# Graph layer in fp32 by split matmuls: early pieces loaded in halves, residual loads moved, and second-half pieces loaded two by two

## The chip, the cores and the metric

The kernel runs on one core of one Trainium2 chip. The metric is the device time of one execution in microseconds; less is better. The kernel before takes 717.71 us (median of 3 runs, 717.27 to 717.86).

## The reference

```python
h = jnp.maximum(_layernorm(x, axis=-1), 0.0)          # x: 8192 x 128, eps 1e-5
x = x + (0.9 * (adj @ h) + 0.1 * L0_gnn_h)            # adj: 8192 x 8192, all float32
```

The work is one product of an 8192 x 8192 matrix with an 8192 x 128 matrix in float32. `adj` alone is 268 MB and is read once.

## The kernel before

The output is computed transposed: 16 chunks of 512 output rows, each chunk one PSUM bank of 128 x 512. `adj` arrives in 256 **pieces** of 128 x 2048 floats (1 MB), numbered q. Pieces 0 to 127 are **wide**: a piece is one block of 128 nodes for four of the first eight chunks, so that block k needs only h of block k, and two pieces use one block. Pieces 128 to 255 are **tall**: a piece is four blocks for one chunk, 16 pieces to a chunk. All of h is made during the wide half.

A float32 product is made from three faster ones. For every piece from 2 on, ScalarE writes `a_hi`, the piece rounded to fp32r (L270), and VectorE writes `a_lo = raw - a_hi` (L316, `low_a`). h is split in the same way into `h_hi` and `h_lo`. TensorE then does 12 matmuls of 512 columns for a piece: four of `h_hi` with `a_hi`, four of `h_lo` with `a_hi`, four of `h_hi` with `a_lo` (L406, L412, L417 in the wide half; L428, L429, L433 in the tall one). Pieces 0 and 1 are multiplied in float32 straight from `raw` (L395).

Everything is written out by hand, with one queue of instructions for each engine and semaphores between them:

- SyncE (SP) issues every transfer, in one queue. `raw` has 6 slots. The load of piece q waits until `a_lo` of piece q - 6 is written (L183, `lo_ready`), since both splits read `raw`. Between the pieces SP issues the loads of x (one for a unit of four blocks, 256 KB, at the pieces in `LOAD_X_AT`), the loads of the residual inputs x and L0_gnn_h for chunk n (512 KB, `load_residual`), and the stores.
- `a_hi` and `a_lo` have 3 slots. ScalarE starts on piece q once TensorE is done with piece q - 3 (`piece_used`).
- The residual load n goes to the one buffer `res_sb`; its issue waits until the sum of load n - 1 is made on VectorE (`add_residual`). `RES_LOAD_AT` and `RES_SUM_AT` give the piece at which SP issues the load and the piece after which VectorE makes the sum. SP stands about 6 pieces ahead of VectorE.
- VectorE makes the layernorm statistics after the pieces in `STATS_AT`, in groups of blocks (`GROUPS`: 1, 3, 4, 4, 4, then 8 blocks); GpSimd makes `rstd`; ScalarE scales and clips h (`scale_unit`) and copies it to `h_hi` (`high_h`), VectorE makes `h_lo` (`low_h`).
- `PARTS` says which pieces are loaded and split in parts: 0 and 1 in four, 2 to 9 in two. A part has a semaphore of its own, so that work starts when a part has landed.
- A finished chunk is scaled, added to its residual (`finish`) and stored; `FINISH` lists chunk and piece.

Of the kernel before, what the change touches and what calls it, by code (L numbers as in the profile page):

```python
# [27 lines left out]
PARTS = {0: 4, 1: 4}  # L28
PARTS.update({_q: 2 for _q in range(2, 10)})
PART_SEMS = sum(PARTS.values())  # L30

# [4 lines left out]
GROUPS = [(0, 1), (1, 4), (4, 8), (8, 12), (12, 16)] + [(_b, _b + 8) for _b in range(16, BLOCKS, 8)]  # L36
# [3 lines left out]
STATS_AT, AGGREGATE_AT, SHIFT_AT, SCALE_AT, LOW_H_AT, LOAD_X_AT = {}, {}, {}, {}, {}, {}  # L40
for _g, (_a, _b) in enumerate(GROUPS):
    if _g < 3:
        continue
    _single = _b - _a == UNIT
    _d = 5 if _g == 3 else 2 * _a - 12 if _single else 2 * _a - 19
    for _k in range(_a, _b):
        STATS_AT.setdefault(_d + _k - _a, []).append(_k)
    _end = _d + _b - _a
    AGGREGATE_AT[_end] = _g
    SHIFT_AT[_end + 1] = _g  # L50
    for _u in range(_a // UNIT, _b // UNIT):
        _s = _end + 3 + 2 * (_u - _a // UNIT)
        SCALE_AT[_s], SCALE_AT[_s + 1] = (_u, 0), (_u, 1)
        LOW_H_AT[_s + 2] = _u
        LOAD_X_AT[_d - 1 + 4 * (_u - _a // UNIT)] = _u
# [46 lines left out]
def build(nc, x, adj_wide, adj_tall, res, out):  # L102
# [4 lines left out]
    with ctx:  # L107
# [19 lines left out]
        exponent = sb("exponent", [P, 2 * UNIT])  # L127
        rstd = sb("rstd", [P, BLOCKS])
        shift = sb("shift", [P, BLOCKS])
        warm = sb("warm", [P, SEG], bf16)  # L130
# [3 lines left out]
        part_landed = [sem(f"part_landed{i}") for i in range(PART_SEMS)]  # L134
# [40 lines left out]
        def _(sp):  # L175
# [28 lines left out]
            load_piece(1)  # L204
            load_x(2, UNIT, 2 * UNIT)
            for q in range(NATIVE, PIECES):
# [3 lines left out]
                load_piece(q)  # L210
# [25 lines left out]
        def _(act):  # L236
# [12 lines left out]
            def scale_unit(u, half):  # L249
# [15 lines left out]
            for q in range(NATIVE, PIECES):  # L265
# [6 lines left out]
                if q == 4:  # L272
                    scale_unit(1, 0)
                if q == 5:
                    scale_unit(1, 1)
                if q in SCALE_AT:
                    scale_unit(*SCALE_AT[q])

        @block.vector
        def _(dve):  # L280
# [74 lines left out]
            dve.wait_ge(x_landed[2], 16)  # L355
# [111 lines left out]
```

## Time and profile before

| | before |
|---|---|
| median of 3 runs | 717.71 us |
| the profiled execution | 718.35 us |
| its span (first to last instruction) | 716.6 us |
| TensorE busy | 707.0 us (99%) |
| VectorE busy | 625.0 us (87%) |
| ScalarE busy | 521.3 us (73%) |
| moved by DMA | 285.73 MB, mean 399 GB/s |
| granted TensorE clock, mean | 1.000 |

The profiled execution took 718.35 us, of which 716.6 us are its span and 1.75 us lie around it; it is 0.64 us above the median. TensorE's busy time is modelled from pipelined matmuls: a matmul row says 0.39 us, but they follow each other every 0.227 us. So its gaps are better read from the start times of pieces than from the busy time.

### The profile page before, as it was taken

How to read it: one execution, taken by the hardware profiler on the slowest of the kernel's cores; microseconds unless marked ns; L12 is line 12 of the kernel's file. 1: busy time of each engine (PE TensorE's matmuls, PEld its weight loads, DVE VectorE, ACT ScalarE, POOL GpSimd, SP SyncE). 2: the span in 40 equal slices, each digit the busy share in tenths (PEclk: the TensorE clock that was granted, in tenths of full speed). 3: DMA queues.
4: the chain of work that ended last, by engine and by line, in shares of the span. 5: the costliest groups of instructions: out<-in, count | busy, mean ns of one | idle time of the engine just before them, and what ended most of it. 6: DMA issues, size and time to landing. Idle time of an engine off the chain costs nothing.

```text
span 716.6 us, 7886 instructions
## 1 busy us (share of the span) xinstructions
PE 707.0 (99%) x3076; PEld 575.3 (80%) x3076; DVE 625.0 (87%) x462; ACT 521.3 (73%) x342; POOL 27.6 (4%) x17
## 2 busy tenths in 40 slices
PE   7999999999999999999999999999999999999998
PEld 2777888888888888888888888888888888888886
DVE  3879998998999989998888888888888889888985
ACT  3878877869688796877767676676767767676773
POOL 1001102001020100200000000000000000000000
DMA  8999999999999999999999999999999999999991
GB/s 291 411 418 420 403 419 419 415 422 414 421 411 422 416 415 402 420 421 412 383 398 409 387 395 378 403 397 388 413 387 406 423 418 413 420 415 425 420 422 75
DMA packets 46117, 285.73 MB, mean 399 GB/s; under 512 B 5120, under 2 KB 5632, under 8 KB 14592
## 3 DMA queue, kind: packets, MB, share of 16 engines
q1 hardware_dynamic: 46080, 285.23, 98.2%
q8 instruction: 24, 0.39, 0.2%
q14 instruction: 13, 0.11, 0.0%
HBM read 281.02 MB, written 4.19 MB: 398 GB/s over the span
## 4 chain that ended last, share of the span: by engine, by line
PE 88%; DMA 4%; DVE 3%; issue 2%; ACT 1%; SPq 1%; POOL 0%; DVEq 0%; ACTq 0%
PE acc L428 16%; PE acc L429 16%; PE acc L433 16%; PE acc L417 13%; PE acc L412 13%; PE acc L406 13%; DMA raw<-wide_dram 4%; DVE a_lo L316 2%; SPq L190 1%; ACT a_hi L270 1%; POOL rstd L232 0%; ACT h_full L239 0%; DVE stats L282 0%; SPq L179 0%; DVE h_lo L308 0%
## 5 line engine op out<-in xcount | busy, mean ns | idle before, releaser
L316 DVE TENSOR_TENSOR a_lo<-raw,a_hi 128x2048 fp32r<-128x2048 f32 (+1 forms) x262 | 581.3, 2224 | 65.3 <-ACT a_hi L270 64.8
L270 ACT ACTIVATE a_hi<-raw 128x2048 fp32r<-128x2048 f32 (+1 forms) x262 | 487.7, 1865 | 175.3 <-PE acc L433 90.4
L428 PE MATMUL acc<-a_hi,h_hi 128*128 128x512 f32 x512 | 199.2, 389 | 0.0
L429 PE MATMUL acc<-a_hi,h_lo 128*128 128x512 f32 x512 | 199.2, 389 | 0.0
L406 PE MATMUL acc<-a_hi,h_hi 128*128 128x512 f32 x504 | 135.9, 390 | 3.0 <-ACT a_hi L270 3.0
L417 PE MATMUL acc<-a_lo,h_hi 128*128 128x512 f32 x504 | 135.8, 391 | 1.2 <-DVE a_lo L316 0.8
L433 PE MATMUL acc<-a_lo,h_hi 128*128 128x512 f32 x512 | 136.8, 389 | 0.0
L412 PE MATMUL acc<-a_hi,h_lo 128*128 128x512 f32 x504 | 134.8, 389 | 0.0
L406 PEld LDWEIGHTS acc<-a_hi,h_hi 128*128 128x128 f32 x504 | 94.1, 188 | 25.2 <-issue 2.9
L417 PEld LDWEIGHTS acc<-a_lo,h_hi 128*128 128x128 f32 x504 | 93.9, 188 | 23.8 <-DVE a_lo L316 4.6
L429 PEld LDWEIGHTS acc<-a_hi,h_lo 128*128 128x128 f32 x512 | 96.1, 188 | 20.0
L433 PEld LDWEIGHTS acc<-a_lo,h_hi 128*128 128x128 f32 x512 | 96.1, 188 | 20.0
L428 PEld LDWEIGHTS acc<-a_hi,h_hi 128*128 128x128 f32 x512 | 96.1, 188 | 19.9
L412 PEld LDWEIGHTS acc<-a_hi,h_lo 128*128 128x128 f32 x504 | 94.6, 188 | 19.8
L232 POOL TENSOR_TENSOR rstd<-var_eps,exponent 128x8 f32<-128x8 f32 (+3 forms) x11 | 26.9, 2443 | 267.0 <-DVE var_eps L295 267.0
L239 ACT ACTIVATE h_full<-x_sb,shift,rstd 128x128 f32<-128x128 f32 x63 | 27.2, 480 | 9.4 <-DVE shift L301 9.4
L282 DVE BATCH_NORM_STATS2 stats<-x_sb 128x6 f32<-128x128 f32 x64 | 17.6, 286 | 9.7 <-DMA x_sb<-x_dram 9.7
L335 DVE SCALAR_TENSOR_TENSOR finished<-acc,residual 128x512 f32<-128x512 f32 (+1 forms) x17 | 11.0, 653 | 3.8 <-issue 3.8
L308 DVE TENSOR_TENSOR h_lo<-h_full,h_hi 128x512 fp32r<-128x512 f32 x16 | 10.9, 683 | 0.0
L324 DVE SCALAR_TENSOR_TENSOR residual<-res_sb 128x512 f32<-128x512 f32 x16 | 10.9, 682 | 0.0
L246 ACT ACTIVATE h_hi<-h_full 128x512 fp32r<-128x512 f32 x16 | 10.1, 633 | 0.6
L301 DVE SCALAR_TENSOR_TENSOR shift<-mean_var,rstd 128x8 f32<-128x8 f32 (+2 forms) x10 | 1.6, 164 | 9.3 <-POOL rstd L232 9.3
(15 smaller groups left out, 26.9 us busy)
## 6 DMA issues: line engine op xcount, KB each, us to landing
raw<-tall_dram SPq DMA_DIRECT2D x128, 1024.0 KB, 8.7
raw<-wide_dram SPq DMA_DIRECT2D x118, 1024.0 KB, 9.8
raw<-wide_dram SPq DMA_DIRECT2D x16, 512.0 KB, 12.6
res_sb<-res_dram SPq DMA_DIRECT2D x16, 512.0 KB, 5.6
x_sb<-x_dram SPq DMA_DIRECT2D x15, 256.0 KB, 10.2
out_dram<-finished SPq DMA_DIRECT2D x15, 256.0 KB, 9.1
raw<-wide_dram SPq DMA_DIRECT2D x8, 256.0 KB, 6.4
out_dram<-finished SPq DMA_DIRECT2D x2, 128.0 KB, 1.8
```

The costliest lines, as they stand in the source:

```text
L232: nc.gpsimd.tensor_tensor(rstd[:, a:b], var_eps[:, a:b], exponent[:, 0:b - a], ALU.pow).then_inc(rstd_ready, 1)
L239: last = nc.scalar.activation(h_full[:, in_h(k), :], x_sb[:, in_x(k), :], ACT.Relu, bias=shift[:, k:k + 1], scale=rstd[:, k:k + 1])
L270: nc.scalar.activation(a_hi[:, q % SPLIT_SLOTS, cols], raw[:, q % RAW_SLOTS, cols], ACT.Copy).then_inc(hi_ready, 1)
L282: return nc.vector.bn_stats(stats[:, k, :], x_sb[:, in_x(k), :])
L316: nc.vector.tensor_tensor(a_lo[:, q % SPLIT_SLOTS, cols], raw[:, q % RAW_SLOTS, cols], a_hi[:, q % SPLIT_SLOTS, cols].bitcast(fp32), ALU.s ...
L335: nc.vector.scalar_tensor_tensor(out=finished[:, n % 2, cols], in0=acc[:, c % WIDE, cols], scalar=1.0 - ALPHA, in1=residual[:, n % RES_RIN ...
L406: nc.tensor.matmul(acc[:, quad * QUAD + j, :], h_hi[:, k, :], a_hi[:, slot, cols], start=False, stop=False)
L412: nc.tensor.matmul(acc[:, quad * QUAD + j, :], h_lo[:, k, :], a_hi[:, slot, cols], start=False, stop=False)
L417: last = nc.tensor.matmul(acc[:, quad * QUAD + j, :], h_hi[:, k, :], a_lo[:, slot, cols], start=False, stop=(k == BLOCKS - 1))
L428: nc.tensor.matmul(bank, h_hi[:, k, :], a_hi[:, slot, cols], start=(k == 0), stop=False)
L429: nc.tensor.matmul(bank, h_lo[:, k, :], a_hi[:, slot, cols], start=False, stop=False)
L433: last = nc.tensor.matmul(bank, h_hi[:, k, :], a_lo[:, slot, cols], start=False, stop=(k == BLOCKS - 1))
```

## The change

1. **Parts.** Pieces 0 to 23 are loaded in halves and split into `a_hi` in halves; the quarters of pieces 0 and 1 are gone. The halves lie in an array of their own, in which each is one stretch of memory. VectorE makes `a_lo` in halves only up to piece 5 (`LOW_PARTS`), and in one pass from piece 6 on.
2. **x and h.** All groups have four blocks. The first load of x behind block 3 moves from ahead of piece 2 to ahead of piece 4, the next ones come at pieces 5, 13, 21 and so on, every eight pieces. `high_h` moves one piece behind the scaling, `h_hi` and `h_lo` included for unit 1.
3. **Residuals.** The first eight loads move from pieces 12, 24, ..., 96 to 44, 54, ..., 114, with the sum at the next piece number on VectorE; the later ones come four pieces earlier, their sums six.
4. **Pairs.** In the tall half one transfer of 2 MB brings pieces q and q + 1 (q even) into two neighbouring slots, with one semaphore. It waits for `a_lo` of piece q - 5.
5. **Warm-up.** TensorE's 12 warm-up matmuls of 512 columns become 15 of 256.

```diff
-PARTS = {0: 4, 1: 4}
-PARTS.update({_q: 2 for _q in range(2, 10)})
+EARLY, EARLY_LOW = 24, 6
+PARTS = {_q: 2 for _q in range(EARLY)}
+LOW_PARTS = {_q: 2 for _q in range(EARLY_LOW)}
...
-    RES_LOAD_AT[12 + 12 * _n if _n < RES_RING else _at - 5] = _n
-    RES_SUM_AT[20 + 12 * _n if _n < RES_RING else _at - 2] = _n
-WARM_UP = 12
+    RES_LOAD_AT[44 + 10 * _n if _n < RES_RING else _at - 9] = _n
+    RES_SUM_AT[45 + 10 * _n if _n < RES_RING else _at - 8] = _n
+WARM_UP = 15
...
+        def load_of(q):
+
+            return q if q < WIDE_PIECES else q - q % 2
+
         def wait_landed(engine, q, i):
             if q in PARTS:
-                engine.wait_ge(part_landed[part_number(q, i)], 16)
+                engine.wait_ge(part_landed[q % RAW_SLOTS][i], 16 * landed_turn(q))
             else:
-                engine.wait_ge(raw_landed[q % RAW_SLOTS], 16 * landed_turn(q))
+                engine.wait_ge(raw_landed[load_of(q) % RAW_SLOTS], 16 * landed_turn(load_of(q)))
...
+            def load_two(q):
+                slot = q % RAW_SLOTS
+                sp.wait_ge(lo_ready, low_through(q + 1 - RAW_SLOTS))
+                sp.dma_start(raw[:, slot:slot + 2, :], adj_tall[(q - WIDE_PIECES) // 2, :, :, :]
+                             ).then_inc(raw_landed[slot], 16)
...
-                load_piece(q)
+                if q < WIDE_PIECES:
+                    load_piece(q)
+                elif q % 2 == 0:
+                    load_two(q)
...
             def low_a(q):
-                for i, cols in parts(q):
-                    dve.wait_ge(hi_ready, split_through(q, i))
+                for i, cols in low_parts(q):
+                    dve.wait_ge(hi_ready, split_through(q, i if q in LOW_PARTS else None))
```

**SP's queue at the start.** These are SP's transfers before, from the first one to the second residual load; `128x512`, `128x1024` and `128x2048` on `raw` are a quarter, a half and a whole piece.

```order
L190 DMA raw<-wide_dram 128x512 x4
L179 DMA x_sb<-x_dram 128x512
L190 DMA raw<-wide_dram 128x1024 x4
L179 DMA x_sb<-x_dram 128x512
L190 DMA raw<-wide_dram 128x1024 x12
L190 DMA raw<-wide_dram 128x2048
L179 DMA x_sb<-x_dram 128x512
L190 DMA raw<-wide_dram 128x2048
L179 DMA x_sb<-x_dram 128x512
L190 DMA raw<-wide_dram 128x2048
L195 DMA res_sb<-res_dram 128x1024
L190 DMA raw<-wide_dram 128x2048 x3
```

The first row above is piece 1, the third pieces 2 and 3. This is the same place in the changed queue, from the load of x blocks 1 to 3 to the last half.

```order
L194 DMA x_sb<-x_dram 128x384
L213 DMA raw<-early_dram 128x1024 x6
L194 DMA x_sb<-x_dram 128x512
L213 DMA raw<-early_dram 128x1024 x2
L194 DMA x_sb<-x_dram 128x512
L213 DMA raw<-early_dram 128x1024 x16
L194 DMA x_sb<-x_dram 128x512
L213 DMA raw<-early_dram 128x1024 x16
L194 DMA x_sb<-x_dram 128x512
L213 DMA raw<-early_dram 128x1024 x6
```

Ahead of piece 2 there is one load of x fewer, ahead of piece 13 still one fewer, and no residual load stands among the first 44 pieces.

**VectorE, pieces 3 to 6.** Before, each `a_lo` is written in two halves (`128x1024`), pieces 3, 4 and 5 in the first row and piece 6 in the third:

```order
L316 TENSOR_TENSOR a_lo<-raw,a_hi 128x1024 x6
L282 BN_STATS stats<-x_sb 128x6
L316 TENSOR_TENSOR a_lo<-raw,a_hi 128x1024 x2
L308 TENSOR_TENSOR h_lo<-h_full,h_hi 128x512
L282 BN_STATS stats<-x_sb 128x6
```

Now, from piece 4 on:

```order
L337 TENSOR_TENSOR a_lo<-raw,a_hi 128x1024 x2
L322 SCALAR_TENSOR_TENSOR shift<-mean_var,rstd 128x4
L337 TENSOR_TENSOR a_lo<-raw,a_hi 128x1024 x2
L303 BN_STATS stats<-x_sb 128x6
L337 TENSOR_TENSOR a_lo<-raw,a_hi 128x2048
```

Piece 6, the last row, is now one pass that needs both halves of `a_hi`.

**SP's queue in the tall half.** Before, around the residual load for finish 8 (issued behind piece 188):

```order
L190 DMA raw<-tall_dram 128x2048 [waits lo_ready] x4
L195 DMA res_sb<-res_dram 128x1024 [waits residual_ready]
L190 DMA raw<-tall_dram 128x2048 [waits lo_ready] x3
L199 DMA out_dram<-finished 128x512 [waits finished_ready]
L190 DMA raw<-tall_dram 128x2048 [waits lo_ready] x4
```

Now, around the same load (issued behind the pair 184, 185):

```order
L199 DMA raw<-tall_dram 128x4096 [waits lo_ready] x5
L218 DMA res_sb<-res_dram 128x1024 [waits residual_ready]
L222 DMA out_dram<-finished 128x512 [waits finished_ready]
L199 DMA raw<-tall_dram 128x4096 [waits lo_ready] x3
L218 DMA res_sb<-res_dram 128x1024 [waits residual_ready]
```

A load is now two pieces (`128x4096`), and the residual load and a store stand side by side, where three single pieces stood between them.

## Rows read from the trace of the kernel before

**Rows 1.** Page, part 1: TensorE's busy time, share of the span, instructions.

```profile
PE 707.0 (99%) x3076; PEld 575.3 (80%) x3076; DVE 625.0 (87%) x462; ACT 521.3 (73%) x342; POOL 27.6 (4%) x17
```

**Rows 2.** Five stretches: busy us (x instructions) by engine, clock, DMA share, GB/s.

```profile
0.00:10.00 10.00, 8.41 (x20) 3.02 (x20) 2.11 (x11) 1.28 (x1) 1.33 (x7) 1.00 0.71 207
10.00:20.00 10.00, 6.92 (x21) 3.82 (x22) 6.09 (x16) 6.13 (x8) 2.24 (x2) 1.00 1.03 399
100.00:150.00 50.00, 50.00 (x223) 41.39 (x222) 46.49 (x45) 39.13 (x29) 3.62 (x1) 1.00 1.01 417
400.00:450.00 50.00, 50.00 (x222) 41.42 (x221) 43.33 (x21) 34.91 (x19) 0.00 (x0) 1.00 1.01 387
650.00:700.00 50.00, 50.00 (x222) 41.42 (x221) 43.20 (x21) 34.80 (x20) 0.00 (x0) 1.00 1.02 422
```

**Rows 3.** TensorE in order of time: start us, us, line, shape, count.

```profile
16.31 0.70 PE L406 MATMUL acc<-a_hi,h_hi 128*128 128x512 f32 x2 [2.09 <-ACT a_hi L270]
...
39.87 1.07 PE L406 MATMUL acc<-a_hi,h_hi 128*128 128x512 f32 x4
...
82.17 1.07 PE L406 MATMUL acc<-a_hi,h_hi 128*128 128x512 f32 x4
...
710.49 0.39 PE L428 MATMUL acc<-a_hi,h_hi 128*128 128x512 f32 x1
```

**Rows 4.** ScalarE's splits that waited for a landing; idle before, releaser in brackets.

```profile
15.11 1.06 ACT L270 ACTIVATE a_hi<-raw 128x1024 fp32r<-128x1024 f32 x1 [1.75 <-DMA raw<-wide_dram]
...
16.37 1.06 ACT L270 ACTIVATE a_hi<-raw 128x1024 fp32r<-128x1024 f32 x1 [0.21 <-DMA raw<-wide_dram]
...
18.93 1.06 ACT L270 ACTIVATE a_hi<-raw 128x1024 fp32r<-128x1024 f32 x1 [0.21 <-DMA raw<-wide_dram]
...
20.89 1.06 ACT L270 ACTIVATE a_hi<-raw 128x1024 fp32r<-128x1024 f32 x1 [0.90 <-DMA raw<-wide_dram]
...
43.86 1.92 ACT L270 ACTIVATE a_hi<-raw 128x2048 fp32r<-128x2048 f32 x1 [1.24 <-DMA raw<-wide_dram]
...
47.59 1.91 ACT L270 ACTIVATE a_hi<-raw 128x2048 fp32r<-128x2048 f32 x1 [1.04 <-DMA raw<-wide_dram]
...
60.69 1.92 ACT L270 ACTIVATE a_hi<-raw 128x2048 fp32r<-128x2048 f32 x1 [0.56 <-DMA raw<-wide_dram]
...
63.18 1.92 ACT L270 ACTIVATE a_hi<-raw 128x2048 fp32r<-128x2048 f32 x1 [0.57 <-DMA raw<-wide_dram]
```

**Rows 5.** Waits, whole run: us in total, times, longest; SPq is SyncE's queue.

```profile
ACT a_hi L270 <- DMA raw<-tall_dram: 9.7, 12, 1.2
...
SPq L190 <- DVE a_lo L316: 509.8, 228, 3.6
SPq L195 <- DVE residual L324: 59.0, 13, 6.7
```

**Rows 6.** Single loads issued at 346, 365, 644 us: last number is us to landing.

```profile
raw<-tall_dram SPq DMA_DIRECT2D x1, 1024.0 KB, 6.3
...
raw<-tall_dram SPq DMA_DIRECT2D x1, 1024.0 KB, 5.6
...
raw<-tall_dram SPq DMA_DIRECT2D x1, 1024.0 KB, 12.4
```

**Rows 7.** Piece 253 from split to matmul.

```profile
699.87 1.92 ACT L270 ACTIVATE a_hi<-raw 128x2048 fp32r<-128x2048 f32 x1 [0.80 <-PE acc L433]
...
701.82 2.29 DVE L316 TENSOR_TENSOR a_lo<-raw,a_hi 128x2048 fp32r<-128x2048 f32 x1 [0.43 <-ACT a_hi L270]
...
705.05 0.39 PE L428 MATMUL acc<-a_hi,h_hi 128*128 128x512 f32 x1
```

**Rows 8.** Head: work of VectorE and ScalarE between the pieces.

```profile
16.20 2.49 DVE L316 TENSOR_TENSOR a_lo<-raw,a_hi 128x1024 fp32r<-128x1024 f32 x2 [0.28 <-ACT a_hi L270]
...
23.14 0.86 ACT L239 ACTIVATE h_full<-x_sb,shift,rstd 128x128 f32<-128x128 f32 x2
...
26.70 0.63 ACT L246 ACTIVATE h_hi<-h_full 128x512 fp32r<-128x512 f32 x1
```

More of the change, by code:

```diff
@@ L25 @@
 RAW_SLOTS, SPLIT_SLOTS = 6, 3
[L28 to L30 removed]
+EARLY, EARLY_LOW = 24, 6
+PARTS = {_q: 2 for _q in range(EARLY)}
+LOW_PARTS = {_q: 2 for _q in range(EARLY_LOW)}
+PART = PIECE // 2
 UNIT = 4
@@ L35 @@
 X_RING, H_RING = 6, 4
[L36 to L55, printed above, removed]
+GROUPS = [(0, 1), (1, UNIT)] + [(_b, _b + UNIT) for _b in range(UNIT, BLOCKS, UNIT)]
+LOAD_X_AT = {4: 1}
+STATS_AT, AGGREGATE_AT, SHIFT_AT = {3: list(range(UNIT, 2 * UNIT))}, {3: 2}, {4: 2}
+SCALE_AT, HIGH_H_AT, LOW_H_AT = {5: (1, 0), 6: (1, 1)}, {6: 1}, {7: 1}
+for _u in range(2, UNITS):
+    _d = UNIT * QUADS * _u - 11
+    LOAD_X_AT[_d] = _u
+    for _k in range(UNIT):
+        STATS_AT[_d + _k] = [_u * UNIT + _k]
+    AGGREGATE_AT[_d + 4] = SHIFT_AT[_d + 5] = _u + 1
+    SCALE_AT[_d + 7], SCALE_AT[_d + 8] = (_u, 0), (_u, 1)
+    HIGH_H_AT[_d + 9] = LOW_H_AT[_d + 10] = _u
 FINISH = [(0, WIDE_PIECES), (1, WIDE_PIECES + 3)]
@@ L88, in split_through, with low_parts, low_through, low_part_of @@
     return sum(PARTS.get(k, 1) for k in range(NATIVE, q)) + own
+def low_parts(q):
+    n = LOW_PARTS.get(q, 1)
+    width = PIECE // n
+    return [(i, slice(i * width, (i + 1) * width)) for i in range(n)]
+def low_through(q, i=None):
+    own = LOW_PARTS.get(q, 1) if i is None else i + 1
+    return sum(LOW_PARTS.get(k, 1) for k in range(NATIVE, q)) + own
 def part_of(q, seg):
     return seg * PARTS.get(q, 1) // QUAD
+def low_part_of(q, seg):
+    return seg * LOW_PARTS.get(q, 1) // QUAD
 def pieces_of_chunk(c):
@@ L126, in build @@
         var_eps = sb("var_eps", [P, BLOCKS])
-        exponent = sb("exponent", [P, 2 * UNIT])
+        exponent = sb("exponent", [P, UNIT])
         rstd = sb("rstd", [P, BLOCKS])
         shift = sb("shift", [P, BLOCKS])
-        warm = sb("warm", [P, SEG], bf16)
+        warm = sb("warm", [P, SEG // 2], bf16)
         acc = ctx.enter_context(nc.psum_tensor("acc", [P, WIDE, SEG], fp32))
         x_landed = [sem(f"x_landed{n}") for n in range(UNITS + 1)]
-        part_landed = [sem(f"part_landed{i}") for i in range(PART_SEMS)]
+        part_landed = [[sem(f"part_landed{s}_{i}") for i in range(2)] for s in range(RAW_SLOTS)]
         raw_landed = [sem(f"raw_landed{s}") for s in range(RAW_SLOTS)]
@@ L156, in landed_turn @@
         def landed_turn(q):
-            return sum(1 for k in range(q % RAW_SLOTS, q + 1, RAW_SLOTS) if k not in PARTS)
+            return sum(1 for k in range(q % RAW_SLOTS, q + 1, RAW_SLOTS) if (k in PARTS) == (q in PARTS))
+        def load_of(q):
+            return q if q < WIDE_PIECES else q - q % 2
         def wait_landed(engine, q, i):
             if q in PARTS:
-                engine.wait_ge(part_landed[part_number(q, i)], 16)
+                engine.wait_ge(part_landed[q % RAW_SLOTS][i], 16 * landed_turn(q))
             else:
-                engine.wait_ge(raw_landed[q % RAW_SLOTS], 16 * landed_turn(q))
+                engine.wait_ge(raw_landed[load_of(q) % RAW_SLOTS], 16 * landed_turn(load_of(q)))
         def in_x(k):
@@ L203, in _ @@
             load_x(1, 1, UNIT)
-            load_piece(1)
-            load_x(2, UNIT, 2 * UNIT)
-            for q in range(NATIVE, PIECES):
+            for q in range(1, PIECES):
                 if q in LOAD_X_AT:
@@ L354, in _ @@
             make_shift(1)
-            dve.wait_ge(x_landed[2], 16)
-            for k in range(UNIT, 2 * UNIT):
-                last = statistics(k)
-            last.then_inc(stats_ready, 1)
-            aggregate(2)
             low_h(0)
@@ L389, in _ @@
             for _ in range(WARM_UP):
-                nc.tensor.matmul(acc[:, WIDE - 1, :], warm[:, 0:P], warm[:, :], start=True, stop=True)
+                nc.tensor.matmul(acc[:, WIDE - 1, 0:SEG // 2], warm[:, 0:P], warm[:, :], start=True, stop=True)
             pe.wait_ge(first_h_ready, 1)
@@ L453 @@
         "x_dram": np.ascontiguousarray(x.reshape(BLOCKS, P, F).transpose(1, 0, 2)),
-        "wide_dram": adj_wide,
+        "early_dram": adj_early,
+        "wide_dram": np.ascontiguousarray(adj_wide[EARLY:]),
         "tall_dram": adj_tall,
```

36 lines of the change are left out of this document (15 added, 21 removed).

## The prediction, on record before the run

> **What bounds the kernel now.** I read the page first. TensorE is busy for 99% of the span [rows 1], so only two things can be won: the time before its matmuls run back to back, and the tail. The windows show where it is not full: 8.41 and 6.92 us of 10 in the first two stretches of 10 us, then 50.00 of 50 [rows 2]. The DMA tells the other half: it moves 207 GB/s in the first 10 us, 399 in the next, later up to 422, always with a busy share near 1. It is close to its own limit, so both limits must be followed.
>
> Next the start times of pieces on TensorE [rows 3]. The last piece (255) starts at 710.49, piece 24 at 82.17: 628.32 us for 231 pieces, 2.720 us each. That is 12 matmuls at 0.227 us, and nothing is lost there. Ahead of it something is. Piece 2 starts at 16.31 and piece 10 at 39.87; eight pieces need 21.76 us, so 1.80 us are lost. From piece 10 to 24 it is 42.30 against 14 x 2.72 = 38.08: 4.22 us lost. So the head costs 16.31 us to its first split matmul and 6.02 us of stalls; this is all that the change can win from. The tail behind the last piece is not touched.
>
> ScalarE says what the head waits for [rows 4]. Each of these splits starts as its data land. Landings give the price of a transfer in a full queue: a half 16.37 - 15.11 = 1.26 us, a whole piece 63.18 - 60.69 = 2.49, a piece and a residual load 47.59 - 43.86 = 3.73, so the residual 1.24; a half and a load of x 20.89 - 18.93 = 1.96, so x 0.70. A piece needs 2.49 us of DMA and 2.72 of TensorE: once the head is over, DMA gains 0.23 us per piece. The head is bound by landings.
>
> **The change, part by part.** *Start.* One load of x fewer stands ahead of piece 2: -0.70 us. The quarters of pieces 0 and 1 (2 MB) become halves. No row has the price of a quarter in a full queue; the first 10 us move half of what later ones do [rows 2], but most of that is the start itself. From below it is nothing, from above the 2 MB at 207 instead of 399 GB/s would be 5 us. I take 0.5, since the halves at 1.26 us are only 1% over a whole piece and a row of half that length should be a few per cent over. Piece 2 then starts 1.2 us earlier, at 15.1. The warm-up costs nothing: TensorE waited 2.09 us for ScalarE ahead of piece 2 [rows 3], and float32 matmuls that run slower in the head are hidden up to that.
>
> *Pieces 2 to 9.* Their landings move with the start, but the second load of x comes ahead of piece 5 and not 11, so from piece 5 to 10 only 0.5 us is left of the 1.2. And the low split is one pass from piece 6 on. A pass of a half costs 2.49 / 2 = 1.25 us [rows 8], a whole one 2.29 [rows 7], and the whole one starts only when both halves of `a_hi` are made. I follow the queues. The second half of piece 2 lands at 16.37 - 1.2 = 15.2; eight halves and two loads of x later, at 26.7, that of piece 6. ScalarE has scaled two blocks (0.86, [rows 8]) behind piece 5 and ends `a_hi` of piece 6 near 28.1; the low pass ends near 30.5. TensorE started piece 6 near 27.6 and wants `a_lo` 1.81 us later, at 29.4: 1.1 us lost. For piece 7 there are 0.86 for two blocks and a copy of four more ahead of `a_hi`: 0.8 lost. For piece 8 VectorE has the low part of h as well: 0.4. With 0.85, 0.3 and 0.5 for the landings of the halves of pieces 2, 4 and 5, the stretch loses 3.9 us where 1.80 are lost now: +2.1.
>
> *Pieces 10 to 23.* The residual load at piece 12 is gone (1.24), the one at 24 too, and one load of x by piece 13 (0.70), another by 16. Piece 13 landed at 47.59 and lands near 47.59 - 1.2 - 1.24 - 0.70 + 0.2 = 44.7 (the 0.2 for halves instead of whole pieces). It now starts 1.97 us after its landing, at 49.56. Following TensorE's own pace from piece 10 (near 40.8) piece 13 starts at 49.0, more than 4 us after its landing. The landings drop out as the bound, and the gap grows by 0.23 us a piece. Of the 4.22 us I keep 0.4 for hitches of VectorE, which has many small passes: -3.8. Groups of four blocks instead of eight add only small instructions to engines that are 73 and 87% busy [rows 1]. The sum for the head is -1.2 + 2.1 - 3.8 = -2.9 us.
>
> *Residuals later on.* SP stood still for 59.0 us, in 13 waits of up to 6.7, because a residual load waited for the sum of the one before [rows 5]. With the sum right behind, this wait is gone. TensorE lost nothing by it after piece 24, so it is worth nothing by itself, but the queue stays fuller. In the wide half eight loads, one per 10 pieces instead of 12, need 10 x 2.49 + 1.24 + 1.25 x 0.70 = 27.0 us of DMA per 27.2 of TensorE. That just fits.
>
> *Pairs.* What a load may take is read at the end [rows 7]. ScalarE starts piece 253 at 699.87, once piece 250 is done; VectorE ends its low pass at 704.11; TensorE starts it at 705.05. So a low pass ends 0.94 us ahead of its piece's start, and ScalarE wants a piece 5.18 us ahead of it. Piece q is issued when the low pass of q - 6 ends, and is wanted 6 x 2.72 + 0.94 - 5.18 = 12.1 us later. A pair is issued one piece later and its even piece is wanted at the same time: 9.4 us. Another 2.7 us may pass until TensorE stands still, since ScalarE and VectorE are ahead. Single loads took from 5.6 to 12.4 us, the long ones late in the run [rows 6]; already now ScalarE waits 12 times for tall loads, 9.7 us in all [rows 5]. A pair has 2.49 us more to move: 8.1 at best.
>
> Three pairs fill the slots. Two slots are filled again after its landing, `a_hi` (1.92), two low passes (4.58) and about 0.1; with 8.1 to land this is 14.7 us, and it must go into 6 x 2.72 = 16.32. In the stretch from piece 184 to 247, a residual load and a store (half its size, 0.62) come every eight pieces: 1.86 x 6 / 8 = 1.4 us more, 16.1 in all. It fits by 0.2 us. Before, each slot was released alone and held less. If a landing takes 6.3 for a single piece, as another row has it, the sum is 16.8, 0.5 too much, and 64 pieces are 10.7 rounds: +5.3 us. So the price lies between 0 and 5.3; the row of 5.6 is the nearest to an empty queue, but residual load and store come at once, 1.86 us in a round that has 0.2 to spare on average, so I take +1.0.
>
> The Trainium skill speaks to this in "DMA: Bandwidth & Descriptors", section "Anatomy of one DMA": a fixed cost near 2.0 us plus the bytes at 436 GB/s, so that large transfers are better used. By it a 1 MB load takes 4.4 us and a pair 6.8, as an estimate. The shortest row here is 1.2 us over that, so I do not use it; by it pairs would cost nothing and the sum would be 714.8. Against the change speaks the section on why a DMA increments its semaphore by 16: only the full count says that data are there. This is what takes the even piece's head start away, and the 9.4 us above are worked out with it.
>
> **Sum.** -2.9 + 1.0 = -1.9 us. The profiled execution took 718.35 with a span of 716.6; it would take 716.45 with a span of 714.7. The median is 0.64 lower: 717.71 - 1.9 = 715.8.
>
> **The rivals.** *Pairs cost nothing* (22%): the transfer of 2 MB lands in 8.1 us or less. For it: the row of 5.6, and that DMA kept 422 GB/s to the end [rows 2]. It gives 714.8; with a start that gains 2 us instead of 1.2, 714.0. *Pairs give all of the gain back* (17%): the rounds are 0.2 to 0.3 us too long, 2 to 3.5 us of stalls: 717 to 718.3. *Slower* (16%): pairs land in 8.8 us or more. It decides from about 8.7 us on (16.7 a round, 0.4 too much, +4.1). Place: TensorE's first matmuls of even pieces from 202 on, waiting for ScalarE, and it for the DMA. For it: single loads took 10 to 12.4 us there. Against it: these are queue, and a shallower queue is what pairs have. It gives 719.9 to 721. *The head's gain does not come* (7%): the later start of `a_lo` costs as much as the landings give, so 717.5. The forecast itself, 715.0 to 716.9, has 38%.
>
> **How the numbers follow.** The bound for faster and slower is 0.2%, 1.44 us, about what a measurement of this kernel can tell: below 716.3 and above 719.1. Faster: 22 for the first rival and 28 of the forecast's 38, 0.50. Slower: 16, and 6 of the cases between, 0.22. Same: 0.28. The range leaves out one in ten on each side: 713.9, the first rival with a better start, to 720.0 within the slower one.
>
> **What would show it.** Right: piece 24 starts near 79.3 on TensorE; stalls of about 1 us at pieces 7 and 8 from VectorE's low pass; no wait for `wide_dram` after piece 12; SP's wait for the residual sum almost zero; pair landings of 8 to 10 us, waits of ScalarE for `tall_dram` above 9.7 us in total, and TensorE's idle time behind piece 200 about 1 us. Wrong: if piece 24 starts later than 81, the head failed; if pieces 184 to 255 take more than 196.8 us (72 x 2.72 = 195.8), pairs cost more than I took.

## The result, and the profile after

The changed kernel takes 723.51 us (median of 4 runs, 721.73 to 724.97) against 717.77 (717.27 to 717.86): a ratio of 1.008, 95% interval 1.0057 to 1.0104. It is slower, where 1.9 us faster was forecast. Its runs also lie further apart: 3.2 us from the lowest to the highest, where those of before span 0.6. The profiled execution took 721.73 us, its span is 719.9; it is the fastest of the four, 1.8 us under the median.

The page of the changed kernel, where it answers to [rows 1], [rows 5] and [rows 6]: busy times; GB/s in 40 slices of 18 us; ScalarE's split, with its idle time and what ended it; the transfers, with the median from issue to landing.

```profile
PE 709.8 (99%) x3079; PEld 574.1 (80%) x3079; DVE 622.7 (86%) x470; ACT 518.3 (72%) x356; POOL 40.6 (6%) x23
...
GB/s 343 410 408 413 419 420 419 421 419 417 421 420 420 419 419 420 419 421 422 381 396 384 383 390 392 392 388 400 421 416 405 423 371 410 409 369 393 382 393 108
...
L293 ACT ACTIVATE a_hi<-raw 128x2048 fp32r<-128x2048 f32 (+1 forms) x276 | 485.3, 1778 | 185.5 <-DMA raw<-tall_dram 104.3
...
raw<-tall_dram SPq DMA_DIRECT2D x64, 2048.0 KB, 10.0
...
res_sb<-res_dram SPq DMA_DIRECT2D x16, 512.0 KB, 11.1
```

The rate holds 417 to 422 GB/s from the fifth slice to the end of the wide half. Where the tall half begins it falls to 381 to 400, and the later slices but the last lie between 369 and 423. The fall is no sign of a slow DMA: a piece of 1.049 MB every 2.720 us is 386 GB/s, and that is all that a full TensorE takes there. The kernel before moved 387 from 400 to 450 us [rows 2]. ScalarE's idle time now ends mostly with a landing of a tall pair. A pair needs 10.0 us from issue to landing.

TensorE in order of time, as in [rows 3]: piece 2, the `a_lo` matmuls of pieces 6 and 7, and the first rows of pieces 10, 24, 184 and 255.

```profile
12.49 0.70 PE L418 MATMUL acc<-a_hi,h_hi 128*128 128x512 f32 x2
...
27.27 1.19 PE L429 MATMUL acc<-a_lo,h_hi 128*128 128x512 f32 x4 [0.58 <-DVE a_lo L337]
...
30.60 1.20 PE L429 MATMUL acc<-a_lo,h_hi 128*128 128x512 f32 x4 [0.30 <-DVE a_lo L337]
...
37.36 1.07 PE L418 MATMUL acc<-a_hi,h_hi 128*128 128x512 f32 x4
...
75.68 1.07 PE L418 MATMUL acc<-a_hi,h_hi 128*128 128x512 f32 x4
...
510.88 0.39 PE L440 MATMUL acc<-a_hi,h_hi 128*128 128x512 f32 x1
...
713.80 0.39 PE L440 MATMUL acc<-a_hi,h_hi 128*128 128x512 f32 x1
```

Read against 2.720 us a piece: piece 2 starts at 12.49 instead of 16.31. From 2 to 10 TensorE takes 24.87 us, 3.11 more than 21.76. From 10 to 24 it takes 38.32, 0.24 more than 38.08. Piece 24 starts 6.49 us earlier than before. From 24 to 184 it is 435.20 us for 160 pieces, 2.720 each and no loss. From 184 to 255 it is 202.92 us for 71 pieces that need 193.12: **9.80 us lost**, all of it behind piece 184, in the stretch with the residual loads. The sum -6.49 + 9.80 = +3.31 us is the difference of the spans (719.9 - 716.6 = 3.3).

Waits of the changed kernel over the whole run (total, times, longest), against [rows 5]:

```profile
ACT a_hi L293 <- DMA raw<-tall_dram: 104.3, 57, 4.1
...
ACT a_hi L293 <- DMA raw<-early_dram: 8.0, 25, 1.0
...
SPq L218 <- DVE residual L345: 0.8, 3, 0.3
```

ScalarE waits 57 times for tall landings, 104.3 us, where it was 12 times and 9.7. SP's wait for the residual sum is gone: 0.8 us where it was 59.0.

Three stretches of the changed kernel, in the columns of [rows 2]:

```profile
0.00:10.00 10.00, 7.84 (x26) 4.28 (x27) 2.44 (x13) 1.87 (x3) 1.97 (x8) 1.00 0.81 290
...
450.00:500.00 50.00, 50.00 (x223) 41.39 (x221) 42.21 (x21) 34.06 (x19) 0.00 (x0) 1.00 1.00 393
...
600.00:650.00 50.00, 48.51 (x205) 37.24 (x203) 40.50 (x22) 32.44 (x18) 0.00 (x0) 1.00 0.99 400
```

The first 10 us now move 290 GB/s (207 before). From 450 to 500 TensorE is full at 393 GB/s; from 600 to 650 it is busy for 48.51 of 50 and does 205 matmuls where 222 fit.

### The profile page after: what moved, and what is told of

Its sections match the earlier page's. It is cut to its first block, busy times and chain, and to the rows that moved or that the text cites. A ratio compares the mean times of both kernels' runs of the same rounds, so it can differ in the third digit from the quotient of the medians.

```text
span 719.9 us, 7866 instructions
## 1 busy us (share of the span) xinstructions
PE 709.8 (99%) x3079; PEld 574.1 (80%) x3079; DVE 622.7 (86%) x470; ACT 518.3 (72%) x356; POOL 40.6 (6%) x23
## 4 chain that ended last, share of the span: by engine, by line
PE 68%; DMA 16%; DVE 8%; issue 4%; ACT 3%; SPq 1%; DVEq 0%
PE acc L429 15%; PE acc L418 15%; PE acc L424 15%; DMA raw<-tall_dram 14%; PE acc L445 8%; PE acc L440 7%; PE acc L441 7%; DVE a_lo L337 7%; ACT a_hi L293 3%; DMA raw<-early_dram 2%; SPq L213 1%; DVE finished L356 0%; DVE residual L345 0%; SPq L194 0%; ACT h_full L263 0%
## 5 line engine op out<-in xcount | busy, mean ns | idle before, releaser
L293 ACT ACTIVATE a_hi<-raw 128x2048 fp32r<-128x2048 f32 (+1 forms) x276 | 485.3, 1778 | 185.5 <-DMA raw<-tall_dram 104.3
L256 POOL TENSOR_TENSOR rstd<-var_eps,exponent 128x4 f32<-128x4 f32 (+2 forms) x17 | 40.1, 2357 | 279.3 <-DVE var_eps L316 279.3
L329 DVE TENSOR_TENSOR h_lo<-h_full,h_hi 128x512 fp32r<-128x512 f32 x16 | 10.8, 677 | 2.1 <-ACT h_hi L270 2.1
L322 DVE SCALAR_TENSOR_TENSOR shift<-mean_var,rstd 128x4 f32<-128x4 f32 (+1 forms) x16 | 2.6, 161 | 10.9 <-POOL rstd L256 10.9
## 6 DMA issues: line engine op xcount, KB each, us to landing
x_sb<-x_dram SPq DMA_DIRECT2D x15, 256.0 KB, 11.2
```

Of the source, the lines that this page charges most:

```text
L256: nc.gpsimd.tensor_tensor(rstd[:, a:b], var_eps[:, a:b], exponent[:, 0:b - a], ALU.pow).then_inc(rstd_ready, 1)
L293: nc.scalar.activation(a_hi[:, q % SPLIT_SLOTS, cols], raw[:, q % RAW_SLOTS, cols], ACT.Copy).then_inc(hi_ready, 1)
```

## The experiments

All ratios are to the kernel before, run beside it on the same chip; its median was 717.87 to 718.51 us.

**The pairs alone undone** (a_singles): each tall piece by its own transfer and into its own slot.

```diff
-                elif q % 2 == 0:
-                    load_two(q)
+                load_piece(q)          # 1 MB, waits for the low pass of q - 6
```

> The changed kernel with the pairs alone undone: in the tall half each piece comes by a transfer of 1 MB into its own slot, issued when the low pass of piece q - 6 is done. Theory (the pairs alone cost the time, about 10 us behind piece 128, and the other edits win 6.5 us in the head): 711 to 712 us, no stall of TensorE behind piece 24. Rival (the faster head and the moved residual loads have used up what DMA had to spare, and pairs are only where it shows): 715 to 718 us, with stalls behind piece 184.

712.33 us (712.32 to 712.40), ratio 0.9922 (0.9907 to 0.9937). The theory holds: the other four edits win 5.6 us (the kernel before took 717.98 beside it) and the pairs cost 11.2. The rival, that the faster head used up DMA's reserve, falls.

**What of the pair costs: the late issue, the common landing, or both.** Three kernels keep transfers of 1 MB and take on one trait of the pair, or two.

```diff
 a_late: both transfers issued when the low pass of q - 5 is done; each piece usable by itself
+                sp.wait_ge(lo_ready, low_through(q + 1 - RAW_SLOTS))
+                for k in (q, q + 1):
+                    sp.dma_start(raw[:, k % RAW_SLOTS, :], adj_tall[k - WIDE_PIECES, :, :]
+                                 ).then_inc(raw_landed[k % RAW_SLOTS], 16)
 a_lump: each issued at its own time; the even piece waits for the odd one too
+                if q >= WIDE_PIECES and q % 2 == 0:
+                    engine.wait_ge(raw_landed[(q + 1) % RAW_SLOTS], 16 * landed_turn(q + 1))
 a_latelump: both edits
```

> The changed kernel, but the two pieces of a pair come by two transfers of 1 MB, issued one behind the other at the moment of the pair (low pass of q - 5), each with its own semaphore and usable by itself. Theory that the later issue is what costs: 717 to 721 us, nearly all of the loss. Theory that the common landing costs (the even piece can't be used until the odd one is there): 711 to 713 us. Theory that the transfer of 2 MB with rows of 16 KB is itself slow: 711 to 713 us.

> The changed kernel, but each tall piece comes by its own transfer of 1 MB, issued at its own time (low pass of q - 6), while ScalarE waits for both pieces of a pair before it starts on the even one. Theory of the common landing: ScalarE starts each even piece up to 2.5 us later, two slots come free late together, 714 to 719 us. Theory of late issue, or of a slow transfer of 2 MB: 711 to 713 us, since TensorE's 2.7 us of cover hold.

> The changed kernel with everything of the pairs but the transfer: two transfers of 1 MB (rows of 8 KB) are issued one behind the other when the low pass of q - 5 is done, and ScalarE waits for both before it starts on the even piece. Each of the two waits alone cost nothing (712.3 and 712.4). Theory that together they make a round of three pairs too long (the step of the prediction: 14.7 us and more in 16.3): 717 to 723 us, ScalarE waiting for tall loads about 100 us in all. Rival, the form of the transfer costs: 712 to 714 us.

The late issue alone takes 712.32 us (0.9921, 0.9906 to 0.9936). The common landing alone takes 712.41 (0.9924, 0.9909 to 0.9939). Both together take 722.44 (1.0059, 1.0044 to 1.0074). Each is free and the two together cost 10.1 us. ScalarE's waits for tall landings say the same; these are the rows of a_late, a_lump and a_latelump, one fence each.

```profile
ACT a_hi L293 <- DMA raw<-tall_dram: 5.6, 7, 1.2
```

```profile
ACT a_hi L292 <- DMA raw<-tall_dram: 18.4, 15, 1.8
```

```profile
ACT a_hi L295 <- DMA raw<-tall_dram: 104.3, 57, 4.9
```

a_lump was expected at 714 to 719 us by the theory of the common landing and a_late at 717 to 721 by that of the late issue; both fell as single causes. a_latelump also settles the form of the transfer: it has no transfer of 2 MB and no rows of 16 KB, and it loses nearly all that the changed kernel loses.

**The form of the transfer.** One transfer of 2 MB with rows of 8 KB (the two pieces lie one behind the other in memory), and two transfers of 1 MB with rows of 16 KB, each for half of the partitions.

```diff
 a_rows8
-adj_tall[(q - WIDE_PIECES) // 2, :, :, :]                      # [P, 2, PIECE]: rows of 16 KB
+adj_tall[(q - WIDE_PIECES) // 2, :, :, :].rearrange("two p n -> p two n")
 a_rows16
+                for i, rows in enumerate((slice(0, P // 2), slice(P // 2, P))):
+                    sp.dma_start(raw[rows, slot:slot + 2, :], adj_tall[(q - WIDE_PIECES) // 2, rows, :, :]
+                                 ).then_inc(raw_landed[slot + i], 16)
```

> The changed kernel with one transfer of 2 MB for a pair as before, but the pieces lie one behind the other in memory, so that a row is 8 KB and the transfer has 256 of them and not 128 of 16 KB. Theory that rows of 16 KB are slow (a packet of 16 KB took 666 ns in the stages with stalls where two of 8 KB take 2 x 315): 712 to 714 us. Theory that one transfer of 2 MB is slow whatever its rows, or that the round is too long: 719 to 725 us.

> The changed kernel with a pair brought by two transfers of 1 MB, each for 64 of the 128 partitions with rows of 16 KB, issued together at the moment of the pair; both are waited for. Theory that rows of 16 KB are slow: 719 to 725 us. Theory that it is the size of one transfer: 712 to 714 us. Theory that the round is too long: 719 to 725 us, as with two transfers by pieces.

Rows of 8 KB: 725.18 us (1.0105, 1.0078 to 1.0131; 723.05 to 727.70), no better than rows of 16 KB. So the long rows are not the cause. The other kernel did not test what it was made for: 995.8 us (969.65 to 1003.78). A stretch of it:

```profile
400.00:450.00 50.00, 36.39 (x121) 27.23 (x121) 23.13 (x12) 19.36 (x12) 0.00 (x0) 0.83 1.01 218
```

Here transfers to 64 of the 128 partitions moved 218 GB/s, about half of what transfers to all 128 moved. This hides whatever the rows do, and the run says nothing on them.

**More slots** (a_slots8): pairs by one transfer of 2 MB, with 8 slots.

```diff
-RAW_SLOTS, SPLIT_SLOTS = 6, 3
-X_RING, H_RING = 6, 4
-RES_RING = 8
+RAW_SLOTS, SPLIT_SLOTS = 8, 3
+X_RING, H_RING = 3, 2
+RES_RING = 5
...
-    RES_LOAD_AT[44 + 10 * _n if _n < RES_RING else _at - 9] = _n
+    RES_LOAD_AT[44 + 10 * _n if _n < RES_RING else _at - 7] = _n
```

> The changed kernel, pairs by one transfer of 2 MB included, but with 8 slots of raw instead of 6, so that four pairs make a round: a slot is wanted again after 8 x 2.72 = 21.8 us instead of 16.3. The room comes from the rings of x (3 units instead of 6), of h (2 instead of 4) and of the residual sums (5 instead of 8); residual loads from the sixth on stand 7 pieces ahead of their finish. Theory that the round of three pairs is too long: the loss goes, 711.5 to 713 us, TensorE full behind piece 24. Rival that a transfer of 2 MB is slow in itself (as the 725.2 of the rows of 8 KB might say): 718 to 725 us.

712.12 us (0.992, 0.9905 to 0.9935): the loss is gone, with the same transfer. Its landings, from the list of its issues, and a stretch of it in the columns of [rows 2]:

```profile
raw<-tall_dram SPq DMA_DIRECT2D x64, 2048.0 KB, 10.8
```

```profile
600.00:650.00 50.00, 50.00 (x222) 41.42 (x221) 44.52 (x24) 34.86 (x19) 0.00 (x0) 1.00 1.01 421
```

A pair takes even longer to land than in the changed kernel (10.8 us against 10.0), and yet ScalarE never waits for a tall landing and TensorE is full. DMA moves 421 GB/s where the changed kernel moved 400 in the same stretch; that follows from the pace of TensorE, which was busy for 48.51 of 50 us there, and doesn't explain it. What counts is not how long a pair takes but how much of the round is left for it. This kernel also moved the late residual loads by two pieces. That this alone would have helped is not excluded by it, but a_nores, next, takes nearly all of their bytes away and keeps more than half of the loss.

**Less beside the pairs** (a_nores): the late residual loads cut to 8 of 512 columns.

```diff
-                sp.dma_start(res_sb[:, :, :], res[FINISH[n][0], :, :, :]).then_inc(res_landed, 16)
+                part = SEG if n < RES_RING else 8
+                sp.dma_start(res_sb[:, :, 0:part], res[FINISH[n][0], :, :, 0:part]).then_inc(res_landed, 16)
```

> The changed kernel, pairs included, but the residual loads from the ninth on bring only 8 of 512 columns, so that most of the residual input of those chunks is left out (the sum over all columns is still made). Theory of the round: what stands in the queue beside the pairs decides; without 1.24 us in every eight pieces the loss shrinks from 11 us to 0 to 3: 712 to 715 us. Rival (pairs are slow by themselves, whatever else is in the queue): 719 to 722 us.

718.69 us (1.0019, 1.0002 to 1.0036), with runs from 717.25 to 721.50. By the medians the loss shrinks from 11.2 to about 6.4 us, against 0 to 3 expected; 718.69 lies just below the rival's 719 to 722, and three of the seven runs lie inside. The profiled execution is one of the slower runs (720.79 us). In it TensorE loses 0.81 us from piece 128 to 184 and 7.72 from there to 255, where the changed kernel lost nothing and 9.80. So the theory, that what stands beside the pairs decides, fails: more than half of the loss comes without the residual loads. Its rows, waits and landings:

```profile
ACT a_hi L294 <- DMA raw<-tall_dram: 109.0, 58, 4.0
...
raw<-tall_dram SPq DMA_DIRECT2D x64, 2048.0 KB, 10.0
```

The median over the whole half is the same 10.0 us. From piece 184 on (issues from 497 to 700 us) it is 9.9 where the changed kernel has 10.4: the residual loads add about 0.5 us to a landing, and without them it is still far from the 8.1 that the prediction took.

**Pairs on the kernel before** (b_pairs): nothing but the pairs added.

```diff
-                load_piece(q)
+                if q < WIDE_PIECES:
+                    load_piece(q)
+                elif q % 2 == 0:
+                    load_two(q)
```

> The kernel before with the pairs alone added. Theory that a round of three pairs is too long for its own sake: the loss of about 10 us comes here too, 725 to 728 us. Rival that pairs only hurt since the head is 6.5 us faster and the residual loads stand beside the stores: 718 to 721 us.

724.99 us (1.0101, 1.0063 to 1.0140), a loss of 7.0. It comes without the faster head and without residual loads beside the stores, 4 us smaller than behind them. The pairs are a loss by themselves; the rival (718 to 721) falls, and the theory's 725 to 728 is met at its edge. Its runs span 723.23 to 728.69.

**The low pass in halves up to piece 9** (a_low10), on top of the pairs undone.

```diff
-EARLY, EARLY_LOW = 24, 6
+EARLY, EARLY_LOW = 24, 10
```

> The changed kernel without pairs (712.3 us), and with the low pass in halves up to piece 9 instead of 5. The stalls of TensorE at pieces 6 to 8, which the prediction put on the whole low pass, should go: 710.5 to 711.3 us. Rival (VectorE is busy with h there, and halves cost it 0.2 us more a piece): 712 to 712.6 us.

711.67 us (711.49 to 711.85; 0.9915, 0.9900 to 0.9930), 0.7 us under a_singles (712.33). It is the best version, 6.2 us under the kernel before. The gain is less than expected, between the two: piece 10 starts at 36.16, 1.2 us earlier than in the changed kernel, and 0.7 of that is lost again before piece 11: the `a_lo` matmuls of piece 10, now the first with a whole low pass, wait for VectorE. The stall has moved with the edge.

**The start.** Four kernels on top of a_low10: pieces 0 and 1 in quarters again (a_quarters), the first load of x for unit 1 ahead of piece 2 again (a_xfirst), both (a_qx), and both with the old warm-up (a_qxw).

```diff
+PARTS.update({0: 4, 1: 4})                       # a_quarters, a_qx, a_qxw
-LOAD_X_AT = {4: 1}
+LOAD_X_AT = {2: 1}                               # a_xfirst, a_qx, a_qxw
-WARM_UP = 15
+WARM_UP = 12                                     # a_qxw, with 512 columns
```

> The best version so far (no pairs, low pass in halves up to piece 9, 711.7 us) with pieces 0 and 1 loaded in quarters again. Piece 2 started 3.8 us earlier in the changed kernel where 1.2 were forecast. Theory that the quarters cost the 2.6 us more: piece 2 starts near 15 and the time is 713.5 to 714.5 us. Rival (it is the load of x taken from ahead of piece 2, and the rest): piece 2 starts near 13, 711.7 to 712.5 us.

> The best version so far (711.7 us) with the load of x for unit 1 ahead of piece 2 again instead of piece 4. By the price of a load of x in a full queue, 0.70 us, piece 2 starts 0.7 us later, pieces 2 and 3 with it, and from piece 4 on nothing changes: 711.7 to 712.4 us. Rival (this load holds up more than itself, since it stands in the start of the queue): above 713 us.

> The best version (711.7 us) with both the quarters of pieces 0 and 1 and the early load of x of unit 1 put back. If the two simply add: piece 2 starts at 12.4 + 1.2 + 1.0 = 14.6 and the time is 711.7 + 2.1 + 0.5 = 714.3 us. Rival (together they hold up the start more than apart): piece 2 near 16.3, 715 us or more.

> As the version with quarters and the early load of x, and the warm-up of before as well: 12 matmuls of 512 columns, not 15 of 256. Theory that the warm-up costs nothing (the prediction's step: TensorE waits for data anyway): the same time and start of piece 2 as without, within 0.3 us. Rival: TensorE's float32 matmuls start 0.5 us later and everything with them, 0.5 us or more.

Quarters: 713.76 us (0.9944, 0.9929 to 0.9959), 2.1 us more. Load of x: 712.17 (0.9918, 0.9902 to 0.9935), 0.5 more. Both: 713.47 (0.9935, 0.9917 to 0.9952), 1.8 more. With the old warm-up: 713.57 (0.9938, 0.9922 to 0.9954), no difference, as predicted. In time the two delays do not add up (714.3 was expected of both). Piece 2 starts, in a_low10, a_quarters, a_xfirst, a_qx and a_qxw in this order:

```profile
12.43 0.70 PE L415 MATMUL acc<-a_hi,h_hi 128*128 128x512 f32 x2 [0.33 <-ACT a_hi L290]
```

```profile
13.59 0.70 PE L416 MATMUL acc<-a_hi,h_hi 128*128 128x512 f32 x2 [0.78 <-ACT a_hi L291]
```

```profile
13.42 0.70 PE L415 MATMUL acc<-a_hi,h_hi 128*128 128x512 f32 x2 [1.07 <-ACT a_hi L290]
```

```profile
14.31 0.70 PE L416 MATMUL acc<-a_hi,h_hi 128*128 128x512 f32 x2 [1.43 <-ACT a_hi L291]
```

```profile
14.42 0.70 PE L416 MATMUL acc<-a_hi,h_hi 128*128 128x512 f32 x2 [1.41 <-ACT a_hi L291]
```

At piece 2 they do add up nearly (12.43, + 1.16, + 0.99, and 14.31 with both), but a part of it is covered by later stalls. For the quarters the time is what the theory said (713.5 to 714.5), while piece 2 starts between its place (near 15) and the rival's (near 13). The kernel before started piece 2 at 16.31 [rows 3], still 1.9 us later than a_qxw. Most of this is not the change. b_pairs has the head of the kernel before, instruction by instruction, and in its trace piece 2 starts 1.5 us earlier:

```profile
14.79 0.70 PE L418 MATMUL acc<-a_hi,h_hi 128*128 128x512 f32 x2 [1.31 <-ACT a_hi L282]
```

The changed head scatters in the same way: in the traces of the changed kernel and of a_singles, a_lump, a_latelump and a_rows8 piece 2 starts at 12.33 to 12.49, in those of a_late and a_nores at 13.30 and 13.70. So one trace of a head tells the start of piece 2 no better than to about 1.5 us, and the differences of about 1 us above are single traces too; the times (2.1, 0.5 and 1.8 us, each of four runs) are the firmer numbers. The 0.4 us that are left between b_pairs and a_qxw lie within that.

**The residual loads** (a_resold): a_low10 with the old `RES_LOAD_AT` and `RES_SUM_AT`.

```diff
-    RES_LOAD_AT[44 + 10 * _n if _n < RES_RING else _at - 9] = _n
-    RES_SUM_AT[45 + 10 * _n if _n < RES_RING else _at - 8] = _n
+    RES_LOAD_AT[12 + 12 * _n if _n < RES_RING else _at - 5] = _n
+    RES_SUM_AT[20 + 12 * _n if _n < RES_RING else _at - 2] = _n
```

> The best version (711.7 us) with the residual loads and sums where they were: from piece 12 on every twelve, and 5 and 2 pieces ahead of the finish later. The prediction's step: each residual load in the head holds up the landings by 1.24 us, and the landings bound TensorE up to piece 23. Behind the faster start this should still cost 0.5 to 2 us: 712.2 to 713.7 us. Rival (the head is now bound by landings of pieces 2 to 6 and later loads are covered): 711.5 to 712.1 us.

714.09 us (0.9946, 0.9931 to 0.9962): the old places cost 2.4 us, more than the 0.5 to 2 expected. A stretch of it:

```profile
40.00:60.00 20.00, 19.13 (x83) 15.17 (x82) 17.33 (x18) 16.65 (x20) 0.20 (x1) 1.00 1.03 409
```

TensorE is busy for 19.13 of 20 us there, and for all 20 in a_low10. By the start times, a_resold loses 1.45 us at piece 13 (a_low10: 0.15), the one behind the first residual load, and 0.53 and 0.50 at pieces 25 and 27, behind the second (a_low10: nothing). The first is close to the 1.24 us that the prediction gave a residual load. The residual loads in the head cost landings, as it had it.

**Pairs with slots enough, and the halves** (a_slots8_low10): the edits of a_slots8 and of a_low10 (`EARLY_LOW` = 10) together.

> Pairs with 8 slots (712.1 us) and the low pass in halves up to piece 9 as in the best version. If the tall half is free of stalls either way, this gives the same as single loads: 711.2 to 712.0 us. Rival (pairs with slots enough are better than single loads): below 711.2.

711.87 us (0.9916, 0.9900 to 0.9931), the same as a_low10 within their runs (711.74 to 712.12 and 711.49 to 711.85). Once ScalarE waits for no tall landing, pairs win nothing.

## Why the prediction was wrong, step by step

**What bounds the kernel**: right in what there was to win. TensorE loses nothing from piece 24 to 184 at 2.720 us a piece, before and after, so it was the head. The reading of the DMA share was weak: the share was not always near 1 (0.71 in the first 10 us), and a share near 1 does not say that DMA is at its limit. [rows 2] has 1.01 at 387 GB/s and 1.02 at 422.

**The start, -1.2 us**: the sign right, the size too small. Piece 2 starts 3.82 us earlier than in the trace before, 2.3 earlier than in that of b_pairs, which has the same head. The load of x was priced at 0.70 and measured 0.99 at piece 2, 0.5 in the time. The quarters were priced at 0.5 and measured 1.16 at piece 2, 2.1 in the time. The first 10 us moved 207 GB/s before, 290 after; the upper bound of 5 us for quarters held, the value was taken too near the lower one. About 1.5 of the 3.82 us is what two traces of one head differ by.

**Pieces 2 to 9, +2.1**: TensorE lost 3.11 us there, where 3.9 were worked out (it was 1.80 before, so +1.3). It lost them where the prediction said. By start times pieces 2, 4 and 5 lose 0.55, 0.24 and 0.52 us (0.85, 0.3 and 0.5 were worked out), pieces 6, 7 and 8 lose 0.90, 0.61 and 0.28 (1.1, 0.8 and 0.4). The mechanism is in the rows: VectorE's whole low pass is what the `a_lo` matmuls of pieces 6 and 7 wait for.

```profile
24.92 2.29 DVE L337 TENSOR_TENSOR a_lo<-raw,a_hi 128x2048 fp32r<-128x2048 f32 x1 [1.24 <-ACT a_hi L293]
28.25 2.29 DVE L337 TENSOR_TENSOR a_lo<-raw,a_hi 128x2048 fp32r<-128x2048 f32 x1 [0.83 <-ACT a_hi L293]
```

The pass of piece 6 starts at 24.92 and ends at 27.21; the matmuls start at 27.27, after 0.58 us in which TensorE was idle. Halves there gain 0.7 us in the end (a_low10).

**Pieces 10 to 23, -3.8**: right, 0.24 us lost against the 0.4 kept. How much of it is the residual loads is known only behind the faster start: there their old places cost 2.4 us, about 1.3 of it at piece 13 and 1.1 behind piece 24 (a_resold), so it doesn't split the 3.8. One sign was wrong: ScalarE was to wait for no `wide_dram` load after piece 12, and it waits 14 times, 7.8 us in all, which costs TensorE nothing. By the traces the head gave 6.49 us, not 2.9, and 2.6 of the 3.6 between are in the first term, a part of them luck of the trace before; by the times of a_singles the four edits gave 5.6.

**Pairs, +1.0**: this is the step that failed, and in it the term for the landing. The mechanism was the one named: a round of three pairs has 16.32 us, of which `a_hi` (1.92), two low passes (4.58) and 0.1 are not the transfer's, so 9.7 are left for issue to landing. I took the shortest landing of a single load (5.6 us), added 2.49 for the second piece and had 8.1, with 0.2 to spare after the residual load and the store. The landings of the changed kernel, issued from 371 to 497 us (no residual loads) and from 497 to 700 (with them):

```profile
raw<-tall_dram SPq DMA_DIRECT2D x23, 2048.0 KB, 9.8
raw<-tall_dram SPq DMA_DIRECT2D x36, 2048.0 KB, 10.4
```

The 8.1 us are real: it is the median of the first five pairs, issued from 344 to 371 us. But they do not last. ScalarE in the stretch from 397 us on, where no residual loads come:

```profile
397.53 1.92 ACT L293 ACTIVATE a_hi<-raw 128x2048 fp32r<-128x2048 f32 x1 [1.43 <-DMA raw<-tall_dram]
399.62 1.92 ACT L293 ACTIVATE a_hi<-raw 128x2048 fp32r<-128x2048 f32 x1 [0.17 <-PE acc L445]
402.73 1.92 ACT L293 ACTIVATE a_hi<-raw 128x2048 fp32r<-128x2048 f32 x1 [1.19 <-DMA raw<-tall_dram]
405.06 1.92 ACT L293 ACTIVATE a_hi<-raw 128x2048 fp32r<-128x2048 f32 x1 [0.41 <-PE acc L445]
408.01 1.92 ACT L293 ACTIVATE a_hi<-raw 128x2048 fp32r<-128x2048 f32 x1 [1.04 <-DMA raw<-tall_dram]
```

Every even piece starts with a landing (idle 1.43, 1.19 and 1.04 us), every odd one with TensorE; the landings come 5.20 and 5.28 us apart, and TensorE has no stall yet. The round is full here. Behind piece 184 it is too long. This is one round there, of pieces 186 and 187: issue, `a_hi` of 186 at the landing, both low passes, and the issue of the next pair into the same slots.

```profile
503.17 0.33 SPq L199 DMA_DIRECT2D raw<-tall_dram  x1
514.01 1.92 ACT L293 ACTIVATE a_hi<-raw 128x2048 fp32r<-128x2048 f32 x1 [3.13 <-DMA raw<-tall_dram]
515.97 4.49 DVE L337 TENSOR_TENSOR a_lo<-raw,a_hi 128x2048 fp32r<-128x2048 f32 x2 [1.16 <-ACT a_hi L293]
520.49 0.33 SPq L199 DMA_DIRECT2D raw<-tall_dram  x1
```

It takes 17.32 us: 10.84 until ScalarE starts and 6.48 from there to the next issue. Over all rounds that start with a pair from 184 to 248 the mean is 17.28, of which 10.55 is the landing and 6.73 the rest. The prediction had 16.1: 6.6 for the rest, which is right, and 9.5 for a landing with a residual load and a store (8.1 + 1.4). The round is 0.96 us longer than 16.32, about as much as the landing is over 9.5; in 11 rounds that is 10.6 us, of which TensorE stands still for 9.80. The residual loads are not needed for it: b_pairs, a_latelump and a_nores lose 1.54, 1.67 and 0.81 us between pieces 128 and 184, where no residual load comes, and the changed kernel lost nothing there in the one execution that was traced.

That it is the round is shown by four runs. With the common landing alone, each load is issued a piece earlier (2.72 us); with the late issue alone, the even piece can be used when its own 1 MB has landed, about 2.5 us ahead of the other. Neither loses anything. With both traits 10.1 us are lost, and with one pair more of slots nothing again, at a landing of 10.8 us.

The wrong bound has a cause in how it was made. 5.6 us was the single best row of the run; the median of single loads lay at 6.7 to 11.7 in stretches of 50 us from 350 to 700, and I read the rest as queue that a shallow ring would not have. But a pair's own queue is always there: it is issued 5.44 us behind the one before, which then has more than 4 us of its 10 to go. With the median of all single loads, 8.7 us, the sum would have been 11.2; the measured 10.0 lies between the two, which fits a shallower queue, but one that shortens the landing less than I took.

Why a landing goes up from 8.1 to 9.8 us at about 371 us, and stays there with no residual load in the queue, is open. DMA is not counted idle there, as this row of the changed kernel shows, in which it moves little:

```profile
388.76:390.12 1.36, 1.36 (x8) 1.13 (x7) 1.36 (x1) 1.36 (x1) 0.00 (x0) 1.00 0.99 253
```

The share is 0.99 while only 253 GB/s move. No run here says what it waits for.

**The landing by a formula.** By the Trainium skill, "DMA: Bandwidth & Descriptors", section "Anatomy of one DMA — SWDGE (gpsimd) path", a transfer of 2 MB takes 6.8 us, as an estimate. The formula is fitted to transfers that GpSimd issues, while SyncE issues all of them here. It was not used for the sum, and the measured median is 3.2 us above it. What the prediction drew from it, that larger transfers are better used, found no gain here: with slots enough, pairs and single loads took 711.87 and 711.67 us. The Trainium skill's rule in the section on why a DMA increments its semaphore by 16, that only the full count says that the data are there, is what the program is written by: it waits for 16, and ScalarE starts even pieces at the landing of the pair. No run here tries a smaller count. This common landing was one of the two waits that cost nothing alone.

**The rivals.** The one on the slower side, pairs that land in 8.8 us or more, is what happened, at its place (TensorE's first stall is at piece 187, most of them at and behind 202). It was priced at 719.9 to 721 us and had 16%. The measured 723.51 is above that even though the head gave more than twice what was forecast; with the forecast's head it would have been about 3 us more. The range to 720.0 was too narrow upward, since it was closed by the row of 6.3 us.

## What to carry to other kernels

When two buffers are released, filled and waited for as one, write down the round: landing, use and release of all that a slot sees, against the time in which the ring goes round once. For the landing take two bounds, its best and its median in the loaded queue; if the round fits only with the best, expect it not to fit. Late release and common landing can each be free and cost 1.4% together, so a trial of one of them proves nothing for both. In a start bound by landings, move out of the way what is not needed yet, before making anything faster.

## What the runs showed of the hardware

Transfers of 1 MB to 64 of the 128 partitions moved 216 to 226 GB/s in stretches of 50 us from 350 to 950, against 387 to 422 in a_late for transfers of the same size to all 128 (stretches of 50 us from 350 to 650); the kernel took 995.8 us, and the granted clock was 0.83 in the stretch shown, in which TensorE was busy for 36.39 of 50 us. Rows of 16 KB instead of 8 made no difference that these runs can tell from their spread (medians 723.51 and 725.18 us, with ranges 721.73 to 724.97 and 723.05 to 727.70).
